# Routing the experts' tokens: every expert over all tokens, or seven sorted tiles with one expert each

## Chip, cores and metric

The kernel runs on one core of a Trainium2 chip. The metric is the device time of one execution, in microseconds, less is better. The engines are TensorE (PE), VectorE (DVE), ScalarE (ACT), GpSimd (POOL) and SyncE (SP), which only issues DMAs.

## What is computed

The input is 16 sequences ("images" below) of 512 tokens of 128 channels, all fp32. Two layers follow each other; each normalises x and adds an attention branch and a feed-forward branch to it. The part that matters here is the feed-forward branch of layer 1, a mixture of four experts of which each token uses one:

```python
def _moe(x, ln_w, ln_b, router_w, expert_wv, expert_proj):
    h = _layernorm(x, ln_w, ln_b)
    logits = h @ router_w
    expert_idx = jnp.argmax(logits, axis=-1)
    out = jnp.zeros_like(x)
    for e in range(4):                       # Dff = 512, C = 128
        gv = h @ expert_wv[e]                # 128 -> 2 x 512
        gate_raw, value = jnp.split(gv, 2, axis=-1)
        y = gate_raw * jax.nn.sigmoid(gate_raw) * value @ expert_proj[e]
        out = out + jnp.where((expert_idx == e)[..., None], y, 0.0)
    return out
```

Around it stand, per image: attention A of layer 1 (16 heads of 64, causal), a second attention B of layer 1 inside the feed-forward block (a causal convolution, 16 heads of 8 with rotary positions), whose result goes into `_moe`; and layer 2, a blockwise attention whose result reaches only the last 64 tokens in this form, and a feed-forward block with FP4-rounded operands.

## The kernel before

All weights are loaded and transposed once and stay in SBUF. Then the images pass through a software pipeline with four streams. In one iteration, image i is in `dense` (attention A and the experts), image i+1 in `ahead` (attention B, up to the routing), image i+2 in `early` (norms, convolution, queries and keys of B), and image i-1 in `behind` (layer 2). `pipeline` runs seven such iterations written out (four ahead of the loop, three behind it) and twelve as a hardware loop (`Fori`). The first and last ones lack some streams.

Each stream is cut into steps, functions with names such as `scores`, `gate`, `round_h`, and the constant list `ORDER` gives the order of all steps of an iteration. `walk` goes through that list on every engine, and each engine has its own functions for the steps in which it takes part; so the list fixes the order of the instructions on each engine, and semaphores tie the engines together. An engine does its instructions strictly in its order: a wait holds up all behind it.

An iteration in the order before: `take_over` (DVE copies the finished `xacc` of image i-1 to `xp`), `begin` (DVE copies the routing `hot` and the residual; ACT copies `h2T` to `h2Td`), then eight head pairs of attention A (`kq`, `v`, `scores`, `norm` on POOL, `z`), with attention B's `row_max` (44 units) and layer 2's attention between them. At the last pair begins the second half: `gate` and `value` 0 to 15 and `down` 0 to 3, interleaved with `ao`, with attention B's 44 `exps` and 16 `attend`, with the `early` stream and with layer 2's `round_x`, `gate1`, `up1`, `round_h` and `transpose_hq`. Gates 12 to 15 and `down` 2 and 3 stand behind the last `attend`, among `divide`, `join`, `project_y`, `ln3_*`, `down1`, `transpose3` and `route`, which end the iteration.

The experts: the activations are kept transposed, `h2Td` (128 channels x 512 tokens). Gate n = 4e + c multiplies 128 columns of expert e's weights with all 512 tokens (line 1387), value n likewise (line 1394): 32 fp32 matmuls of 512 columns an image. ACT takes the tanh (729), DVE makes (tanh + 1) x gate (980) and then x value (993), which gives `ym`. `down(e)` (1415) has 16 matmuls of 128 columns per expert, 64 an image, and `expert_acc` (1004) adds the result to `xacc` times the one-hot column `hotd[:, t, e]`. PSUM banks 0 to 2 rotate between gates and values; bank 3 holds `ao` and the downs. `route` (1128 to 1140) makes the one-hot `hot` with some ten tiny DVE operations, each linked to the one before by a semaphore wait.

Other lines of the rows: 1337 `kq`; 1359 and 1362 `scores` on PE, 718 on ACT, 1020 on DVE; 1376 `z`; 614 `norm` on POOL; 1403 `ao`; 1479/1481/760 `exps`; 1494 `attend`; 1314 any transpose of four tiles; 1599, 1604 `gate1`, `up1`; 1609 `transpose_hq`; 1616 `down1`; 1524 `route` on PE; 885 to 901 the nine operations of an FP4 rounding (`round_x`, `round_h`); 1147, 1014, 1015 `take_over` and `begin`; 543 and 549 SyncE's loads of `x`.

## Time and profile before

| | us |
|---|---|
| median of 3 runs (lowest, highest) | 3894.04 (3883.72, 3913.9) |
| the profiled execution's own time | 3885.07 |
| its span, first to last instruction | 3883.0 |
| PE busy | 3406.5 (88%) |
| DVE busy | 2506.9 (65%) |
| ACT busy | 1754.1 (45%) |
| POOL busy | 381.3 (10%) |
| mean granted clock of TensorE | 0.941 of full speed |

Busy means that an instruction of that engine was at work by the profile. PE's matmuls are pipelined and their ends modelled, so a matmul's own duration overlaps the next one's; in the chain of waits the overlap is taken out. An fp32 matmul is two instructions in the records (x2). "PEld" is the loading of the stationary operand.

### The profile page before, as it was taken

How to read it: one execution, taken by the hardware profiler on the slowest of the kernel's cores; microseconds unless marked ns; L12 is line 12 of the kernel's file. 1: busy time of each engine (PE TensorE's matmuls, PEld its weight loads, DVE VectorE, ACT ScalarE, POOL GpSimd, SP SyncE). 2: the span in 40 equal slices, each digit the busy share in tenths (PEclk: the TensorE clock that was granted, in tenths of full speed). 3: DMA queues.
4: the chain of work that ended last, by engine and by line, in shares of the span. 5: the costliest groups of instructions: out<-in, count | busy, mean ns of one | idle time of the engine just before them, and what ended most of it. 6: DMA issues, size and time to landing. Idle time of an engine off the chain costs nothing.

```text
span 3883.0 us, 62655 instructions
## 1 busy us (share of the span) xinstructions
PE 3406.5 (88%) x20319; PEld 1876.6 (48%) x20319; DVE 2506.9 (65%) x5526; ACT 1754.1 (45%) x4156; POOL 381.3 (10%) x676
## 2 busy tenths in 40 slices
PE   2689998989999898999989899898989989898864
PEld 1245455544545455454545545454555545454432
DVE  4555677657767666776766677677667767756453
ACT  0254554535454454545545454544545455454421
POOL 0000200102020010202001020200102020110201
PEclk6799999989999999999989999999999999999975
DMA  4111102020200202020020202002020200200000
GB/s 100 18 25 13 22 2 36 2 37 2 27 11 2 36 2 37 2 29 9 5 33 2 37 2 29 8 7 32 2 37 2 30 7 5 30 1 4 1 3 3
DMA packets 78817, 66.93 MB, mean 17 GB/s; under 512 B 8626, under 2 KB 75124, under 8 KB 78452
## 3 DMA queue, kind: packets, MB, share of 16 engines
q1 hardware_dynamic: 78452, 62.41, 11.2%
q8 instruction: 187, 3.06, 0.4%
q14 instruction: 178, 1.46, 0.1%
HBM read 15.47 MB, written 4.19 MB: 5 GB/s over the span
## 4 chain that ended last, share of the span: by engine, by line
PE 68%; DVE 12%; issue 8%; POOL 6%; ACT 5%; SPq 1%; DMA 1%; POOLq 0%; DVEq 0%; ACTq 0%
PE ps L1376 7%; PE ps L1394 5%; PE ps L1359 5%; PE ps L1387 5%; PE ps L1415 5%; PE ps L1494 4%; PE ps L1479 4%; PE ps L1558 3%; PE ps L1337 3%; PE ps L1580 3%; PE ps L1403 3%; DVE nma L1020 2%; PE ps L1460 2%; PE ps L1349 2%; POOL vn L614 2%
## 5 line engine op out<-in xcount | busy, mean ns | idle before, releaser
L718 ACT ACTIVATE share_a<-ps,nma 128x128 f32<-128x128 f32 (+3 forms) x1024 | 531.3, 524 | 432.3 <-DVE nma L1020 430.2
L1020 DVE TENSOR_REDUCE nma<-ps 128x2 f32<-128x256 f32 (+3 forms) x512 | 420.8, 825 | 416.0 <-PE ps L1362 408.2
L1084 DVE TENSOR_REDUCE nmx<-ps 128x1 f32<-128x384 f32 (+3 forms) x704 | 426.7, 634 | 201.9 <-PE ps L1462 198.2
L760 ACT ACTIVATE share_z<-ps 128x512 f32<-128x512 f32 (+1 forms) x704 | 367.7, 558 | 407.6 <-PE ps L1481 405.4
L614 POOL TENSOR_TENSOR vn<-va,rla 128x512 f32<-128x512 f32 x128 | 133.7, 1044 | 3060.7 <-DVE rla L976 3060.7
L1376 PE MATMUL ps<-share_a,vn 128*64 128x512 f32 (+3 forms) x2048 | 324.1, 461 | 37.1 <-POOL vn L614 35.0
L1337 PE MATMUL ps<-xnTd,wkqT 128*128 128x512 f32 x512 | 279.2, 672 | 70.1 <-issue 47.3
L729 ACT ACTIVATE share_g<-ps 128x512 f32<-128x512 f32 x256 | 153.0, 598 | 361.1 <-PE ps L1387 359.9
L1460 PE MATMUL ps<-kst,qst 96*128 96x128 bf16 (+3 forms) x1024 | 264.5, 311 | 56.1 <-DMA kst<-part 36.4
L1387 PE MATMUL ps<-h2Td,wgv 128*128 128x512 f32 x512 | 267.8, 605 | 2.8 <-ACT share_a L718 2.8
L1394 PE MATMUL ps<-h2Td,wgv 128*128 128x512 f32 x512 | 269.1, 607 | 0.0
L980 DVE SCALAR_TENSOR_TENSOR share_g<-share_g,ps 128x512 f32<-128x512 f32 x256 | 175.5, 686 | 138.5 <-ACT share_g L729 132.8
L1479 PE MATMUL ps<-qst,kst 99*128 99x512 bf16 (+3 forms) x1024 | 253.1, 303 | 12.2 <-ACT share_z L760 8.0
L1415 PE MATMUL ps<-wdn,share_a 128*128 128x128 f32 x2048 | 243.1, 277 | 21.3 <-DVE share_a L993 21.3
L1376 PEld LDWEIGHTS ps<-share_a,vn 128*64 128x64 f32 x2048 | 144.4, 143 | 234.5 <-issue 195.7
L1415 PEld LDWEIGHTS ps<-wdn,share_a 128*128 128x128 f32 x2048 | 236.6, 193 | 43.0 <-issue 33.8
L1359 PE MATMUL ps<-kq_odd 64*128 64x128 f32 (+3 forms) x1024 | 216.7, 501 | 41.6 <-ACT share_a L718 35.5
L993 DVE SCALAR_TENSOR_TENSOR share_a<-share_g,ps 128x512 f32<-128x512 f32 x256 | 175.7, 686 | 105.1 <-PE ps L1394 96.9
L1359 PE MATMUL ps<-share_g 64*128 64x128 f32 (+3 forms) x1024 | 209.7, 486 | 29.9 <-ACT share_a L718 21.3
L718 ACT ACTIVATION_READ_ACCUMULATOR share_a<-ps,nma 128x1 f32 x1024 | 202.5, 198 | 0.0
L1462 PE MATMUL ps<-up_b,ident_b 128*128 128x128 bf16 x1024 | 201.5, 225 | 0.0
L1479 PEld LDWEIGHTS ps<-qst,kst 99*128 99x128 bf16 x1024 | 99.3, 98 | 205.2 <-ACT share_z L760 98.6
(220 smaller groups left out, 5607.3 us busy)
## 6 DMA issues: line engine op xcount, KB each, us to landing
qst<-part SPq DMA_DIRECT2D x144, 128.0 KB
kst<-part SPq DMA_DIRECT2D x144, 128.0 KB
xin<-in_L_attn_x SPq DMA_DIRECT2D x16, 256.0 KB, 12.0
xk<-xn SPq DMA_DIRECT2D x16, 256.0 KB, 18.8
xres<-in_L_attn_x SPq DMA_DIRECT2D x16, 256.0 KB, 2.8
out<-xn SPq DMA_DIRECT2D x16, 256.0 KB, 11.9
wgv<-in_L_ffn_expert_wv SPq DMA_DIRECT2D x1, 2048.0 KB
qst<-share_h SPq DMA_DIRECT2D x48, 16.0 KB, 2.2
```

The source lines that it names most:

```text
L718: activation(pa[:, h % 4, OFF[t]:OFF[t] + P * (t + 1)], ps[:, b + k, 0:P * (t + 1)], ACT.Exp, bias=nma[:, h, t:t + 1], accum_out=la[:, h, ...
L760: activation(pt[:, n % 2, h % 4:h % 4 + k, 0:wd], src, ACT.Exp, scale=SCALE_B)\
L1020: v.tensor_reduce(nma[:, 2 * p:2 * p + 2, t], ps[:, b:b + 2, 0:P * (t + 1)], AX.X, ALU.max, negate=True).then_inc(amax, 1)
L1084: v.tensor_reduce(nmx[:, h:h + k, t], src, AX.X, ALU.max, negate=True).then_inc(bmax_ready, 1)
L1337: ins = mm(ps[:, b + z, :], wkqT[:, z, 2 * DA * p:2 * DA * (p + 1)], xnTd[:, :], start=True, stop=True)
L1359: mm(ps[:, b + k, 0:P * (t + 1)], kq[p % 2][rows, 0, tile(t)], kq[p % 2][rows, 1, 0:P * (t + 1)], start=True, stop=False)
L1376: ins = mm(ps[DA * k:DA * k + DA, 4, 0:P * (t + 1)], vn[:, h % 4, t, :], pa[:, h % 4, OFF[t]:OFF[t] + P * (t + 1)], start=(t == NT - 1), s ...
L1387: mm(ps[:, (2 * n) % 3, :], wgv[:, e, c * P:(c + 1) * P], h2Td[:, :], start=True, stop=True).then_inc(gate_psum, 1)
L1394: mm(ps[:, (2 * n + 1) % 3, :], wgv[:, e, DFF + c * P:DFF + (c + 1) * P], h2Td[:, :], start=True, stop=True).then_inc(value_psum, 1)
L1415: ins = mm(ps[:, 3, tile(t)], ym[:, e % 2, c, tile(t)], wdn[:, e, c, :], start=(c == 0), stop=(c == CHUNKS - 1))
L1460: mm(ps[:, b, o:o + wd], qst[0:SHIFT_ROW, h, tile(t)], kst[0:SHIFT_ROW, h, 0:wd], start=True, stop=False)
L1479: mm(ps[:, b, o:o + wd], kst[0:SHIFT_ROW + PARTS, h, tile(j)], qst[0:SHIFT_ROW + PARTS, h, j * P:T], start=True, stop=False)
```

## The change

Tokens are sorted by their expert into tiles of 128 tokens, each expert's share rounded up to whole tiles. With 512 tokens and 4 experts that is at most `SORTED` = 7 tiles, and always seven are computed. Each tile meets its own expert only, whose number is read from SBUF into a register of PE.

- `rank` (PE, end of the iteration, behind `route`): 8 small bf16 matmuls of the one-hot with a strictly triangular and an all-ones matrix give each token's rank within its expert, and each expert's total, in PSUM bank 5.
- `place` (DVE, right behind it): ten small operations, linked, give each token's row `place_i` in the sorted order and each tile's expert `expert_i`.
- `scatter` (POOL, the last step): four indirect DMAs of 128 rows of 512 bytes write the normalised activations `xh` to `h_sorted` in device memory. SyncE loads them back as `hs` (256 + 192 KB) at the start of the next iteration.
- `begin` copies `place_i` and `expert_i`; ACT's copy `h2Td` is gone.
- `sort` (behind the last `z`): 7 PE transposes of `hs`, two ACT activations with the norm's weight and bias to `hsT`, and seven `value_load`s on PE.
- Per tile j: `gate` and `value`, one matmul of 512 columns each, tokens stationary and the expert's weights moving; tanh and the two DVE operations on 128 x 512 as before; `turn`, four PE transposes and an ACT copy to `ymT`; `down`, four matmuls of 128 columns, and an ACT copy to `ysort`. Gates use banks 2 and 3, values and downs 0 and 1. Both alternate.
- `store_y` (ACT issues it) writes `ysort` to `y_sorted`; `gather` (POOL) has four indirect DMAs that fetch each token's row to `yg`; `take_over` adds `yg` to `xacc` where it copied. `acc` is gone.
- `ORDER` is new throughout. All seven tiles stand ahead of the last ten `exps`; none of the expert work is left behind `attend(3,3)`. `gate1(2)` and `up1(2)` come ahead of `exps 40`. `ln2_stats` moves behind `scores(0,3)`, `ln2_root` behind `z(0)`, `project_v` behind `scores(1,1)`; the row maxima begin behind `scores(2,0)`; the layer 2 attention is spread anew.

The diff, cut to its core:

```diff
+SORTED = NT + EXPERTS - 1
 ...
+    ("take_over",), ("begin",), ("kq", 0), ("v", 0), ("kq", 1), ("scores", 0, 0), ("v", 1), ("scores", 0, 1),
+    ("scores", 0, 2), ("scores", 0, 3), ("ln2_stats",), ("kq", 2), ("scores", 1, 0), ("scores", 1, 1),
+    ("project_v",), ("norm", 0), ("scores", 1, 2), ("z", 0), ("ln2_root",), ("v", 2), ("scores", 1, 3), ("kq",
+    3), ("ln2_apply",), ("transpose2",), ("scores", 2, 0), ("row_max", 0), ("row_max", 1), ("keys1",),
 ...
+    7), ("mix1", 1), ("z", 7), ("sort",), ("project1",), ("round_x", 0), ("load_x",), ("ln0_stats",), ("exps",
+    0), ("exps", 1), ("ln0_root",), ("ln0_apply",), ("ln1_apply",), ("ao",), ("add_ao",), ("gate", 0),
+    ("value", 0), ("gate", 1), ("exps", 2), ("exps", 3), ("value", 1), ("round_x", 1), ("turn", 0),
+    ("round_x", 2), ("round_x", 3), ("round_x", 4), ("exps", 4), ("attend", 0, 0), ("exps", 5), ("exps", 6),
+    ("down", 0), ("gate", 2), ("exps", 7), ("transpose1",), ("value", 2), ("exps", 8), ("exps", 9), ("turn",
 ...
+    26), ("round_h", 0, 0), ("round_h", 0, 1), ("round_h", 0, 2), ("round_h", 0, 3), ("attend", 2, 0),
+    ("exps", 27), ("exps", 28), ("round_h", 0, 4), ("down", 3), ("gate", 5), ("value", 5), ("exps", 29),
+    ("turn", 4), ("exps", 30), ("exps", 31), ("attend", 2, 1), ("down", 4), ("transpose_hq", 0), ("gate", 6),
+    ("gate1", 1), ("value", 6), ("turn", 5), ("up1", 1), ("round_h", 1, 0), ("exps", 32), ("down", 5),
+    ("turn", 6), ("attend", 2, 2), ("exps", 33), ("attend", 2, 3), ("round_h", 1, 1), ("down", 6),
+    ("store_y",), ("round_h", 1, 2), ("round_h", 1, 3), ("round_h", 1, 4), ("exps", 34), ("exps", 35),
+    ("transpose_hq", 1), ("exps", 36), ("exps", 37), ("gate1", 2), ("exps", 38), ("attend", 3, 0), ("exps",
+    39), ("up1", 2), ("exps", 40), ("exps", 41), ("attend", 3, 1), ("exps", 42), ("exps", 43), ("attend", 3,
+    2), ("attend", 3, 3), ("turn_x",), ("round_h", 2, 0), ("round_h", 2, 1), ("round_h", 2, 2), ("round_h", 2,
+    3), ("round_h", 2, 4), ("transpose_hq", 2), ("gather",), ("divide", 0), ("divide", 1), ("gate1", 3),
+    ("divide", 2), ("divide", 3), ("up1", 3), ("round_h", 3, 0), ("round_h", 3, 1), ("round_h", 3, 2),
+    ("round_h", 3, 3), ("join",), ("project_y",), ("round_h", 3, 4), ("transpose_hq", 3), ("ln3_stats",),
+    ("ln3_root",), ("ln3_apply",), ("down1",), ("transpose3",), ("route",), ("rank",), ("place",),
+    ("scatter",),
 ...
+                def load_sorted():
+                    sp.wait_ge(scattered, count(i, AHEAD["scattered"], 16 * NT))
+                    sp.dma_start(hs, h_sorted.rearrange("(t p) c -> p t c", p=P)).then_inc(hs_loaded, 16)
 ...
+                def scatter():
+                    pool.wait_ge(placed, count(nxt, AHEAD["placed"], 1))
+                    if type(nxt[0]) is not int or nxt[0] + nxt[1]:
+                        pool.wait_ge(scatter_turn, count(nxt, AHEAD["scatter_turn"], 0))
+                    if i is not None:
+                        pool.wait_ge(hs_loaded, count(i, DENSE["hs_loaded"], 16))
+                    nc.gpsimd.tensor_tensor(turn_s[:, :], vones[0:1, VCOLS - 1:VCOLS],
+                                            vones[0:1, VCOLS - 1:VCOLS], ALU.mult).then_inc(scatter_turn, 1)
+                    for t in range(NT):
+                        nc.gpsimd.indirect_dma_start(
+                            h_sorted, bass.IndirectOffsetOnAxis(place_i[:, t:t + 1].bitcast(U32), 0),
+                            xh[:, t, :], None).then_inc(scattered, 16)
+
+                def gather():
+                    pool.wait_ge(y_stored, count(i, DENSE["y_stored"], 16))
+                    if type(i[0]) is not int or i[0] + i[1]:
+                        pool.wait_ge(gather_turn, count(i, DENSE["gather_turn"], 0))
+                    nc.gpsimd.tensor_tensor(turn_g[:, :], vones[0:1, VCOLS - 1:VCOLS],
+                                            vones[0:1, VCOLS - 1:VCOLS], ALU.mult).then_inc(gather_turn, 1)
+                    for t in range(NT):
+                        nc.gpsimd.indirect_dma_start(
+                            yg[:, t, :], None, y_sorted,
+                            bass.IndirectOffsetOnAxis(placed_d[:, t:t + 1].bitcast(U32), 0)).then_inc(y_gathered, 16)
 ...
+                def sort():
+                    act.wait_ge(hs_psum, count(i, DENSE["hs_psum"], 1))
+                    act.wait_ge(zav_done, count(i, DENSE["zav_done"], PAIRS))
+                    activation(hsT[:, 0:T], ps[:, 0, :], ACT.Identity, bias=ln1[:, 3:4], scale=ln1[:, 2:3])\
+                       .then_inc(hsT_ready, 1)
+                    activation(hsT[:, T:SORTED * P], ps[:, 1, 0:SORTED * P - T], ACT.Identity, bias=ln1[:, 3:4],
+                               scale=ln1[:, 2:3]).then_inc(hsT_ready, 1)
+
+                def gate(j):
+                    act.wait_ge(gate_psum, count(i, DENSE["gate_psum"], j + 1))
+                    if j >= 2:
+                        act.wait_ge(moe_y, count(i, DENSE["moe_y"], j - 1))
+                    activation(sg[:, j % 2, :], ps[:, GATE_BANK[j % 2], :], ACT.Tanh, scale=0.5)\
+                       .then_inc(silu_done, 1)
+
+                def turn(j):
+                    act.wait_ge(yT_psum, count(i, DENSE["yT_psum"], j + 1))
+                    if j >= 2:
+                        act.wait_ge(down_psum, count(i, DENSE["down_psum"], j - 1))
+                    copy(ymT[:, j % 2, :, :].rearrange("p c t -> p (c t)"), ps[:, GATE_BANK[j % 2], :])\
+                       .then_inc(yT_ready, 1)
+
+                def down(j):
+                    act.wait_ge(down_psum, count(i, DENSE["down_psum"], j + 1))
+                    copy(ysort[:, j, :], ps[:, VALUE_BANK[j % 2], 0:C]).then_inc(y_ready, 1)
+
+                def store_y():
+                    act.wait_ge(y_ready, count(i, DENSE["y_ready"], SORTED))
+                    if prv is not None:
+                        act.wait_ge(y_gathered, count(prv, DENSE["y_gathered"], 16 * NT))
+                    act.dma_start(y_sorted.rearrange("(t p) c -> p t c", p=P), ysort).then_inc(y_stored, 16)
 ...
+                    v.tensor_copy(placed_d[:, :], place_i[:, :])
+                    v.tensor_copy(expert_d[:, 0:SORTED], expert_i[:, 0:SORTED])
 ...
+                def place():
+                    dve.wait_ge(rank_psum, count(nxt, AHEAD["rank_psum"], 1))
+                    if i is not None:
+                        dve.wait_ge(carried, count(i, DENSE["carried"], 1))
+                        dve.wait_ge(scattered, count(i, AHEAD["scattered"], 16 * NT))
+                    rank = ps[:, 5, 0:NT * EXPERTS].rearrange("p (t e) -> p t e", e=EXPERTS)
+                    total = ps[:, 5, NT * EXPERTS:(NT + 1) * EXPERTS]
+                    wide_lg = lg[:, :, :]
+                    begun = rb[:, :, :]
+                    link_a(v.tensor_tensor(wide_lg, total.unsqueeze(2).to_broadcast([P, EXPERTS, NT]),
+                                           sizes.rearrange("p (e n) -> p e n", e=EXPERTS), ALU.is_gt))
+                    link_a(v.tensor_tensor(begun, flat(lg).unsqueeze(1).to_broadcast([P, EXPERTS, EXPERTS * NT]),
+                                           below, ALU.mult))
+                    link_a(v.tensor_reduce(first[:, :], begun, AX.X, ALU.add))
+                    link_a(v.scalar_tensor_tensor(out=place_f[:, :, :],
+                                                  in0=first[:, :].unsqueeze(1).to_broadcast([P, NT, EXPERTS]),
+                                                  scalar=float(P), in1=rank, op0=ALU.mult, op1=ALU.add))
+                    link_a(v.tensor_tensor(place_f[:, :, :], place_f[:, :, :], hot[:, :, :], ALU.mult))
+                    link_a(v.tensor_reduce(lmax[:, :], place_f[:, :, :], AX.X, ALU.add))
+                    link_a(v.tensor_copy(place_i[:, :], lmax[:, :]), False)
+                    late = rb[:, :, :].rearrange("p a b -> p (a b)")[:, 0:SORTED * 3].rearrange(
+                        "p (n e) -> p n e", e=3)
+                    link_a(v.tensor_tensor(late, tiles.unsqueeze(2).to_broadcast([P, SORTED, 3]),
+                                           first[:, 1:EXPERTS].unsqueeze(1).to_broadcast([P, SORTED, 3]), ALU.is_ge))
+                    link_a(v.tensor_reduce(expert_f[:, 0:SORTED], late, AX.X, ALU.add))
+                    v.tensor_copy(expert_i[:, 0:SORTED], expert_f[:, 0:SORTED]).then_inc(placed, 1)
 ...
                 def take_over():
-                    dve.wait_ge(moe_acc, count(prv, DENSE["moe_acc"], EXPERTS))
+                    dve.wait_ge(ao_added, count(prv, DENSE["ao_added"], 1))
+                    dve.wait_ge(y_gathered, count(prv, DENSE["y_gathered"], 16 * NT))
                     if type(prv[0]) is not int or prv[0] + prv[1]:
                         dve.wait_ge(out_ready, count(prv, BEHIND["out_ready"], 0))
-                    link_b(v.tensor_copy(xp[:, :, :], xacc[:, :, :]))
+                    link_b(v.tensor_tensor(xp[:, :, :], xacc[:, :, :], yg[:, :, :], ALU.add))
 ...
+                expert = {}
+
+                def sort():
+                    pe.wait_ge(carried, count(i, DENSE["carried"], 1))
+                    pe.wait_ge(hs_loaded, count(i, DENSE["hs_loaded"], 16))
+                    pe.wait_ge(aexp_done, count(i, DENSE["aexp_done"], 4 * HEADS))
+                    for j in range(SORTED):
+                        ins = tr(ps[:, j // NT, tile(j % NT)], hs[:, j, :], idn)
+                    ins.then_inc(hs_psum, 1)
+                    for j in range(SORTED):
+                        expert[j] = pe.value_load(expert_d[0:1, j:j + 1], min_val=0, max_val=EXPERTS - 1)
+
+                def gate(j):
+                    if j == 1:
+                        pe.wait_ge(ao_added, count(i, DENSE["ao_added"], 1))
+                    elif j:
+                        pe.wait_ge(yT_ready, count(i, DENSE["yT_ready"], j - 1))
+                    pe.wait_ge(hsT_ready, count(i, DENSE["hsT_ready"], j // NT + 1))
+                    mm(ps[:, GATE_BANK[j % 2], :], hsT[:, tile(j)],
+                       wgv[:, bass.ds(expert[j], 1), 0:DFF].rearrange("c a f -> c (a f)"),
                        start=True, stop=True).then_inc(gate_psum, 1)
 
-                def value(n):
-                    e, c = n // CHUNKS, n % CHUNKS
-                    if n:
-                        pe.wait_ge(gate_read, count(i, DENSE["gate_read"], n))
-                    mm(ps[:, (2 * n + 1) % 3, :], wgv[:, e, DFF + c * P:DFF + (c + 1) * P], h2Td[:, :],
+                def value(j):
+                    if j < 2:
+                        pe.wait_ge(hsT_ready, count(i, DENSE["hsT_ready"], 2))
+                    else:
+                        pe.wait_ge(y_ready, count(i, DENSE["y_ready"], j - 1))
+                    mm(ps[:, VALUE_BANK[j % 2], :], hsT[:, tile(j)],
+                       wgv[:, bass.ds(expert[j], 1), DFF:2 * DFF].rearrange("c a f -> c (a f)"),
                        start=True, stop=True).then_inc(value_psum, 1)
+
+                def turn(j):
+                    pe.wait_ge(moe_y, count(i, DENSE["moe_y"], j + 1))
+                    for c in range(CHUNKS):
+                        ins = tr(ps[:, GATE_BANK[j % 2], tile(c)], ym[:, j % 2, tile(c)], idn)
+                    ins.then_inc(yT_psum, 1)
+
+                def down(j):
+                    pe.wait_ge(yT_ready, count(i, DENSE["yT_ready"], j + 1))
+                    for c in range(CHUNKS):
+                        ins = mm(ps[:, VALUE_BANK[j % 2], 0:C], ymT[:, j % 2, c, :],
+                                 wdn[:, bass.ds(expert[j], 1), c, :].rearrange("p a c -> p (a c)"),
+                                 start=(c == 0), stop=(c == CHUNKS - 1))
+                    ins.then_inc(down_psum, 1)
 ...
+                def rank():
+                    pe.wait_ge(hot_ready, count(nxt, AHEAD["hot_ready"], 1))
+                    some = lambda a, b: hot[:, a:b, :].rearrange("p t e -> p (t e)")
+                    mm(ps[:, 5, 0:NT * EXPERTS], strict_b[:, :], some(0, NT), start=True, stop=False)
+                    for t in range(1, NT):
+                        mm(ps[:, 5, t * EXPERTS:NT * EXPERTS], ones_b[:, :], some(0, NT - t), start=False,
+                           stop=(t == NT - 1))
+                    for t in range(NT):
+                        ins = mm(ps[:, 5, NT * EXPERTS:(NT + 1) * EXPERTS], ones_b[:, :], some(t, t + 1),
+                                 start=(t == 0), stop=(t == NT - 1))
+                    ins.then_inc(rank_psum, 1)
```

## Rows read from the trace of the kernel before

**Rows 1.** The page, part 2: tenths busy in 40 equal slices; PEclk the granted clock.
```profile
PE   2689998989999898999989899898989989898864
...
PEclk6799999989999999999989999999999999999975
```

**Rows 2.** SyncE's lines 543 and 549: min/median/max ns, first and last start.
```profile
L543 SPq DMA_DIRECT2D xin<-in_L_attn_x x16: 384/397/879, 42.6 to 3098.0; - x16
L543 SPq FUSED_REGOPS  x12: 51/51/58, 612.1 to 3097.8; - x12
L543 SPq MOVE xin<-in_L_attn_x x12: 35/38/38, 612.2 to 3097.9; - x12
...
DMA to landing us min/median/max: 2.7/12.0/18.0
...
L549 SPq DMA_DIRECT2D xres<-in_L_attn_x x16: 372/373/4366, 89.7 to 3329.5; - x16
```

**Rows 3.** Busy time by stretch of one iteration, and of the closing stage.
```profile
core 0: us, PE busy (x) PEld busy (x) DVE busy (x) ACT busy (x) POOL busy (x), PEclk, DMA share, GB/s
1520.34:1533.00 12.66, 9.44 (x44) 5.59 (x44) 2.60 (x14) 2.93 (x4) 0.00 (x0) 0.87 0.46 82
1533.00:1642.30 109.30, 98.76 (x585) 50.00 (x587) 73.16 (x127) 63.89 (x173) 23.82 (x42) 1.00 0.01 2
1642.30:1713.50 71.20, 70.84 (x479) 39.71 (x479) 52.42 (x118) 34.92 (x68) 0.00 (x0) 1.00 0.02 4
1713.50:1746.30 32.80, 26.37 (x165) 19.71 (x164) 26.30 (x85) 7.10 (x14) 0.00 (x0) 0.95 0.62 77
...
3733.00:3883.00 150.00, 64.65 (x146) 29.93 (x146) 50.16 (x110) 21.10 (x37) 15.48 (x34) 0.57 0.01 4
```

**Rows 4.** The chain of waits in order of time: start, us, what.
```profile
1501.08 0.86 PE ps L1387 x2
...
1520.32 9.42 issue
...
1671.67 3.57 PE ps L1415 x32
```

**Rows 5.** Timeline of PE: start, us, what, and the idle time before it.
```profile
1534.39 0.92 PE L1359 MATMUL ps<-share_g 64*128 64x384 f32 x4 [1.62 <-ACT share_a L718]
...
1662.39 0.60 PE L1314 MATMUL ps<-ident,xh 128*128 128x128 f32 x4
1662.83 1.02 PE L1394 MATMUL ps<-h2Td,wgv 128*128 128x512 f32 x2
...
1737.66 2.94 PE L1616 MATMUL ps<-wdT,share_s 128*128 128x128 f32 x24 [0.57 <-ACT share_s L822]
...
3687.78 0.76 PE L1599 MATMUL ps<-wguT,share_s 128*128 128x352 f32 x2
...
3707.84 1.92 PE L1394 MATMUL ps<-h2Td,wgv 128*128 128x512 f32 x2
...
3719.04 0.86 PE L1599 MATMUL ps<-wguT,share_s 128*128 128x352 f32 x2
```

**Rows 6.** Timeline of DVE at the restart and in the tail after it.
```profile
1529.92 0.43 DVE L1147 COPY xp<-xacc 128x512 f32<-128x512 f32 x1 [9.59 <-issue]
...
1533.07 1.02 DVE L1020 TENSOR_REDUCE nma<-ps 128x2 f32<-128x256 f32 x2
...
1732.35 0.51 DVE L885 TENSOR_REDUCE qm<-share_s 128x22 f32<-128x352 f32 x1
...
1735.96 0.53 DVE L901 TENSOR_TENSOR share_q<-share_s,qm 128x352 f32<-128x352 f32 x1
...
1744.79 0.17 DVE L1135 TENSOR_TENSOR hot<-lg,taken 128x4 f32<-128x4 f32 x1
```

**Rows 7.** Groups of instructions by line and shape: busy us, mean ns.
```profile
L993 DVE SCALAR_TENSOR_TENSOR share_a<-share_g,ps 128x512 f32<-128x512 f32 x256 | 175.7, 686 | 105.1 <-PE ps L1394 96.9 <-DVE ry L869 3.6
...
L729 ACT ACTIVATE share_g<-ps 128x512 f32<-128x512 f32 x256 | 153.0, 598 | 361.1 <-PE ps L1387 359.9
...
L1004 DVE SCALAR_TENSOR_TENSOR xacc<-ps,hotd,xacc 128x128 f32<-128x128 f32 x256 | 71.8, 345 | 1.8 <-PE ps L1415 1.8
```

257 lines of the change are left out of this document (122 added, 135 removed), and 12 rows, old and new, of the table ORDER.

## The prediction

> **What bounds the kernel now.** I read the page's slices first. TensorE (PE) is busy 8 or 9 tenths of nearly every slice at a granted clock of 0.9 [rows 1]. A loop iteration lasts 226.0 us: SyncE's line 543 runs twelve times in the loop, from 612.1 to 3097.8 us, so 2485.7 / 11 [rows 2]. One iteration, cut into stretches [rows 3]:
> - A, the restart of the loop (12.7 us) and attention A with the row maxima and layer 2 (109.3 us). PE works 9.4 and 98.8 us of it.
> - B, from the last head pair to the end of `attend(3,3)`, 71.2 us, PE busy 70.8. Nothing but less PE work shortens it.
> - C, the tail, where PE has 26.4 and DVE (VectorE) 26.3 of 32.8 us. DVE's last operation of it ends at 1744.96, 31.5 us after its start at 1713.5 [rows 6].
>
> Between a tail and the next A, DVE stands still for 9.59 us with "issue" as the cause, and the chain of waits runs through that gap with 9.42 us [rows 4, 6]. 
>
> **PE work.** The chain of waits gives times net of overlap: an fp32 matmul of 512 columns is 0.86 us (two instructions), 16 of 128 columns are 3.57 us, 0.223 each [rows 4]. Four transposes start at 1662.39 and the next work at 1662.83: 0.11 each [rows 5]. Per image the change makes
> - gate and value: 32 matmuls become 14, -18 x 0.86 = -15.5 us
> - down: 64 become 28, -36 x 0.223 = -8.0
> - transposes: 7 in `sort`, 4 in each of 7 `turn`, 35 x 0.11 = +3.9
> - `rank`: 8 small bf16 matmuls, in no row; with the transposes as the nearest, 8 x 0.11 = +0.9; ends 0 and, at 0.223, 1.8.
>
> Net -18.7 us an image. That is the ceiling, reached only where PE sets the end. The seven tiles are a constant of the code, so no data makes them fewer.
>
> **B.** PE now has 11 gates, 12 values and `down` 0 and 1 in it: 23 x 0.86 + 2 x 3.57 = 26.9 us; the other gates and downs stand in C. After, all expert work is in B: 14 x 0.86 + 28 x 0.223 + 35 x 0.11 = 22.1; `gate1(2)`, `up1(2)` (352 columns, 0.59 each by the 512's 0.86) and three transposes come forward, 1.5. B loses 3.3 us. Three costs are unknown:
> - Seven `value_load`s stand in PE's queue between `sort` and `ao`. From below: 0.035 us each, SyncE's MOVE, hidden under the transposes queued ahead, so 0. From above: 4.37 us, the longest that an instruction with an address from a register held SyncE (line 549), 30.6 in all. The nearest row is the median of such an instruction, 0.397: I take 0.4 each and no cover, +2.8 us [rows 2]. The Trainium skill (DMA: Bandwidth & Descriptors, Latency and other measured facts) gives some 600 ns as the floor of a `tensor_load`; if this is one, the estimate is 4.2 us and the sum 21 us more, which no row here shows.
> - 42 matmuls take their weights' address from a register: 51 + 38 ns of register work each [rows 2], 3.7 us on PE's sequencer. It hides behind matmuls of 0.22 to 0.86 us: 0, at most 3.7.
> - A tile becomes a chain: gate 0.86, tanh 0.60, two DVE operations of 0.69, turn 0.44, a copy of 0.60, down 0.89, a short copy: 5 us, some 6 with the handovers [rows 4, 5, 7]. Two tiles are in flight, so seven need 21 us of 70; but `down(5)`, `turn(6)`, `down(6)` stand close together. I take 2 us of stalls; 0 to 8, the upper end one more chain and a third without cover.
>
> ScalarE loses 16 tanh and the `h2Td` copy and gains 7 tanh, 2 activations, 7 copies like a tanh and 7 short ones: 10 us against 12, on an engine busy 35 of 71 us here [rows 3]: nothing. B: -3.3 + 2.8 + 2.0 = +1.5 us.
>
> **C.** DVE has few gaps here, and PE will have about 11 us of work, so DVE's list is the length. It loses four gate and four value operations (0.65 from start to start, 5.2 us), two `acc` (eight of line 1004, 2.1 with overlap), `up1(2)` (two operations of 352 columns, 1.0) and most of `round_h(2)`, nine operations, 1732.35 to 1736.40 in the fourth: 4.1 us, of which some 3.1 can run from `exps 40` on, within B. It gains the wait for `rank` (0.9) and `place`, ten small operations, each linked to the last, 0.2 us apart like those of `route` (the last takes 0.17): 2.0 [rows 6, 7]. -11.4 + 2.9 = -8.5 us. `place` stands ahead of the branch, so nothing hides it.
>
> The clock takes some back. Where PE has just waited it runs at the lower level, 1.2 GHz: after 57% of rest in the closing stage the granted clock is 0.57 (between 0.5, 1.2 GHz, and 1, 2.4 GHz), it is 0.87 at the restart, and a value matmul at the lower level takes 1.92 us, not 1.02 [rows 3, 5]. With PE at 11 of 23 us I expect that in the second half of C. On its chain are the end of `down1` (2.94 when fast), `transpose3` and `route`: +2.5 us, 0 to 7 [rows 5]. The Trainium skill (TensorE: Matmul & The Clock Gate, What's actually happening) makes this the rule, the clock is gated unless recent activity releases it, and so speaks against a change that makes PE idler; followed through all of C it gives rival 3.
>
> **A.** PE's work is as it was. DVE ran `take_over`, `begin` and the statistics ahead of the first row maximum, 1529.92 to 1533.07; now the statistics come after the first head pair, `take_over` adds two tensors (0.69 for 0.43) and `begin` has a tiny copy more: 1.5 instead of 3.15 us, -1.6. `ln2_root` moves away from where PE waited 1.62 us for ScalarE [rows 5, 6]: -0.9. Together -2.5, and from -6 to +4, since the order of the whole stretch is new.
>
> **POOL, DMA.** Four indirect DMAs in `scatter`, four in `gather`, in no row. From below 0.38 us each, from above 4.37 [rows 2]; I take 1.0, as software has to do more for them than SyncE at its 0.397. POOL needs its own restart, about DVE's 9.6 us, and `norm(0)` is wanted some 23 us after the tail: 4 + 9.6 fits. `gather` has all of C before `take_over` waits for it; loads of 256 KB land in 12 us at the median [rows 2]. Cost 0; beyond 2.3 us each, `norm(0)` is late by four times the excess. Queued behind `take_over` on DVE are `begin` and every row maximum, so a late gather would stop all of A.
>
> **Sum.** Per iteration +1.5 - 8.5 + 2.5 - 2.5 = -7.0 us. Images 0 to 14: 15 x 7.0 = 105. The last image's dense stage is bound by the layer 2 stream once the gates are gone: its four `gate1` stand at 3687.8 to 3719.0, 10.4 us apart [rows 5]; at the 7 us that DVE's six and the transposes between need, the last comes 11 earlier. Prologue, with `rank` and `place` without cover, a memset and one load: +4. 105 + 11 - 4 = 112. The profiled execution took 3885.1 us (span 3883.0), so 3773. The median of the runs shown, 3894.0, is 9 us above it; I make no correction.
>
> **Rivals.**
> 1. PE sets everything and the new order fills the holes: 16 x 18.7 = 299, 3586 us. For it: PE at 70.8 of 71.2 in B. Against: C is DVE's already, and PE rests 20 us of 226 now.
> 2. PE's sequencer: each `value_load` is a memory round trip, 2.7 us by the shortest landing [rows 2]: 18.9 in place of 2.8, an iteration 9.1 us longer than before: 3885 + 15 x 9.1 + 5 + 4 = 4030 us. It makes the kernel slower from 1.4 us a load. For it: nothing passes them in PE's queue, and `ao` stands behind them. Against: they may run beside the queued transposes.
> 3. The clock eats the gain: PE at 1.2 GHz through all of C. `down1`, `join`, `project_y`, transposes and `route`, 7 us on C's chain, double: +4.5 over the 2.5 counted, and B's tile chains stall 2 us more: -0.5 an iteration, 3870 us. It decides if the clock in C is near 0.5 throughout.
>
> **Chances and range.** Forecast, 3690 to 3840: 0.56. Between it and rival 1, and that: 0.17. Rival 3: 0.14. Rival 2: 0.13. The range, 3640 to 3890, goes halfway to rival 1 and holds rival 3. A measurement of this kernel tells about 1%. Faster by over 1% (below 3855): 0.76. Within 1%: 0.11. Slower: 0.13.
>
> **What would show it.** Right: B near 73 us, with a gap on PE behind the seven transposes; C near 25 us to DVE's last operation, DVE without gaps and PE half busy, clock under 0.95; DVE's "issue" gap near 9.6. Wrong: a PE gap over 8 us ahead of `ao`; `vn` waiting for POOL's own DMA issues; or PE idle all through B, when the tile chain and not PE is the bound.

## The result: slower by 0.9%, outside the predicted range

| | before | after |
|---|---|---|
| median of 7 runs each, us (lowest, highest) | 3905.12 (3883.72, 3913.9) | 3936.14 (3924.51, 3941.98) |
| span of the profiled execution | 3883.0 | 3928.3 |
| PE busy | 3406.5 | 3219.6 |
| DVE busy | 2506.9 | 2305.7 |
| mean granted clock | 0.941 | 0.901 |

The ratio is 1.0089 [1.0064, 1.0113]. The forecast was 3773, in a range of 3640 to 3890. The work did go: 187 us of PE and 201 us of DVE (for PE less than the ceiling of 16 x 18.7 = 299, in part since a matmul lasts longer at a lower clock, `down1` below). The time did not.

The page of the kernel after, part 2, answers to [rows 1]: more slices of 7 on PE, more 8s in the clock.

```profile
PE   2788898978889797988979788897979789797854
...
PEclk7799998989989899999989898998989899999865
```

SyncE's loads of `xin`, which answer to [rows 2]:

```profile
L589 SPq MOVE xin<-in_L_attn_x x12: 35/38/38, 635.6 to 3145.8; - x12
```

Twelve times in the loop, so an iteration is (3145.8 - 635.6) / 11 = 228.2 us; it was 226.0. I call this "the iteration" for every kernel below.

Busy time by stretch, kernel after; columns as in [rows 3]:

```profile
1539.20:1551.20 12.00, 8.74 (x36) 4.74 (x36) 1.04 (x5) 2.51 (x3) 4.10 (x5) 0.78 0.64 111
1551.20:1667.30 116.10, 103.60 (x589) 51.90 (x589) 75.43 (x140) 64.09 (x173) 24.41 (x42) 0.96 0.04 11
1667.30:1741.20 73.90, 68.88 (x491) 41.45 (x491) 48.73 (x110) 39.69 (x81) 4.25 (x6) 0.98 0.04 11
1741.20:1767.40 26.20, 15.22 (x94) 12.69 (x86) 16.87 (x69) 4.22 (x8) 0.00 (x0) 0.72 0.60 78
```

The tail (last row) shrank from 32.8 to 26.2 us, B (third row) grew from 71.2 to 73.9, and the first half (second row) from 109.3 to 116.1, with the granted clock at 0.96 instead of 1.00 in these two iterations (from z(0) to z(7), as means over the loop, 0.96 and 0.98). In the tail the granted clock is 0.72, between its two levels (0.5 and 1); it was 0.95.

The timeline of DVE, kernel after, at the end of the tail and the restart; it answers to [rows 6]:

```profile
1764.74 0.17 DVE L1225 TENSOR_TENSOR hot<-lg,taken 128x4 bf16<-128x4 f32 x1
1765.56 0.17 DVE L1242 TENSOR_TENSOR lg<-ps,tab 128x16 f32<-128x16 f32 x1 [0.65 <-PE ps L1672]
...
1767.40 0.17 DVE L1258 CAST expert_i<-expert_f 128x7 int32<-128x7 f32 x1
1777.61 0.69 DVE L1266 TENSOR_TENSOR xp<-xacc,yg 128x512 f32<-128x512 f32 x1 [10.04 <-issue]
```

The wait for `rank` is 0.65 us and `place` 2.0, as priced; the "issue" gap is 10.04 us.

The timeline of PE, kernel after: at the border from the first half to B, near the end of B, and `down1` in the tail:

```profile
1669.94 0.98 PE L1506 MATMUL ps<-ident,share_r 128*128 128x128 f32 x7
1672.66 0.43 PE L1732 MATMUL ps<-w1T,share_q 128*64 128x128 f32 x2 [1.74 <-issue]
...
1739.43 0.64 PE L1629 MATMUL ps<-share_z,vones 128*32 128x256 f32 x8 [1.18 <-issue]
1740.93 0.43 PE L1629 MATMUL ps<-share_z,vones 128*32 128x128 f32 x8 [0.86 <-ACT share_z L856]
...
1755.62 4.85 PE L1763 MATMUL ps<-wdT,share_s 128*128 128x128 f32 x24 [0.57 <-ACT share_s L920]
```

The gap of 1.74 us behind the seven transposes is where the seven `value_load`s stand. That of 1.18, with 0.86 behind it, stands between the last `attend`s, and nothing that the profile shows ends it.

The loads themselves, kernel after, line 1509 in this one iteration (min/median/max ns, first and last start):

```profile
L1509 PEldq TENSOR_LOAD <-expert_d x7: 295/297/312, 1668.1 to 1672.0; - x7
L1509 PEldq FUSED_REGOPS  x7: 146/146/157, 1668.5 to 1672.4; - x7
```

They start 3.9 / 6 = 0.65 us apart. They begin under `z(7)`, which starts at 1667.63. PE has work until 1672.66 - 1.74 = 1670.92, so 2.8 of their 7 x 0.65 = 4.5 us are covered.

### The profile page after: what moved, and what is told of

Its sections match the earlier page's. It is cut to its first block, busy times and chain, and to the rows that moved or that the text cites. A ratio compares the mean times of both kernels' runs of the same rounds, so it can differ in the third digit from the quotient of the medians.

```text
span 3928.3 us, 61348 instructions
## 1 busy us (share of the span) xinstructions
PE 3219.6 (82%) x19279; PEld 1796.0 (46%) x19279; DVE 2305.7 (59%) x5161; ACT 1779.0 (45%) x4252; POOL 525.9 (13%) x836
## 4 chain that ended last, share of the span: by engine, by line
PE 61%; DVE 14%; issue 10%; ACT 7%; POOL 6%; SPq 1%; DMA 1%; POOLq 0%; another core or an unknown queue 0%; DVEq 0%; ACTq 0%
PE ps L1495 7%; PE ps L1478 6%; PE ps L1629 4%; PE ps L1705 4%; PE ps L1614 4%; PE ps L1550 3%; DVE nma L1109 3%; PE ps L1526 3%; PE ps L1517 2%; POOL vn L662 2%; PE ps L1468 2%; PE ps L1539 2%; PE ps L1456 2%; PE ps L1763 2%; PE ps L1595 2%
## 5 line engine op out<-in xcount | busy, mean ns | idle before, releaser
L1456 PE MATMUL ps<-xnTd,wkqT 128*128 128x512 f32 x512 | 281.3, 676 | 73.9 <-issue 69.1
L662 POOL TENSOR_TENSOR vn<-va,rla 128x512 f32<-128x512 f32 x128 | 145.2, 1135 | 1175.7 <-DVE rla L1078 1175.7
L1629 PE MATMUL ps<-share_z,vones 128*32 128x512 f32 (+3 forms) x2048 | 191.7, 446 | 28.8 <-ACT share_z L856 16.2
L1616 PE MATMUL ps<-low_b,ident_b 128*128 128x128 bf16 x1024 | 195.0, 221 | 0.0
L1468 PE MATMUL ps<-wvT,xnTd 128*128 128x128 f32 x1024 | 152.2, 295 | 23.0 <-ACT share_z L793 22.5
L1705 PE MATMUL ps<-share_q,share_s 128*128 128x512 f32 x256 | 150.9, 673 | 21.8 <-ACT share_s L893 13.8
L1481 PEld LDWEIGHTS ps<-up_b,ident_b 128*128 128x128 bf16 x1024 | 58.6, 98 | 239.5 <-issue 224.6
L1456 PEld LDWEIGHTS ps<-xnTd,wkqT 128*128 128x128 f32 x512 | 97.0, 211 | 152.6 <-issue 141.9
L1468 PEld LDWEIGHTS ps<-wvT,xnTd 128*128 128x128 f32 x1024 | 136.9, 205 | 56.0 <-ACT share_z L793 33.7
## 6 DMA issues: line engine op xcount, KB each, us to landing
xk<-xn SPq DMA_DIRECT2D x16, 256.0 KB, 16.9
```

What stands on the lines that cost most here:

```text
L1456: ins = mm(ps[:, b + z, :], wkqT[:, z, 2 * DA * p:2 * DA * (p + 1)], xnTd[:, :], start=True, stop=True)
L1468: ins = mm(ps[:, 4, tile(t)], xnTd[:, tile(t)], wvT[:, 2 * DA * p:2 * DA * (p + 1)], start=True, stop=True)
L1629: ins = mm(ps[32 * k:32 * k + 32, 4, j * P:T], vones[:, c0:c0 + 32], pt[:, n % 2, k, 0:T - j * P], start=(j == 0), stop=(j == NT - 1))
L1705: mm(ps[:, 7, :], qbd[:, 2 * p:2 * p + 2, :].rearrange("c h q -> c (h q)"), k1T, start=True, stop=False)
```

## The experiments

The table sets all kernels side by side. The stretches are means over 8 to 12 loop iterations of each profile, cut at DVE's first operation of `take_over`, PE's first matmul of `z(0)` and of `z(7)`, PE's first transpose of `turn_x`, and DVE's last operation. z(7) to turn_x is the prediction's B, turn_x to DVE's end its C; the other three columns together are its A. The last column is the mean granted clock of the whole execution.

| kernel | median us | iteration | take_over to z(0) | z(0) to z(7) | z(7) to turn_x | turn_x to DVE's end | DVE's gap | clock |
|---|---|---|---|---|---|---|---|---|
| before | 3905 | 226.0 | 16.5 | 98.3 | 71.6 | 31.2 | 9.0 | 0.941 |
| after | 3936 | 228.2 | 14.4 | 105.1 | 73.8 | 25.1 | 10.6 | 0.901 |
| e1 | 3850 | 224.3 | 17.5 | 99.2 | 72.3 | 25.5 | 10.4 | 0.902 |
| e2 | 3921 | 231.3 | 15.5 | 104.7 | 71.6 | 31.2 | 9.7 | 0.936 |
| e3 | 3879 | 224.7 | 15.2 | 104.7 | 71.8 | 24.8 | 10.0 | 0.929 |
| e4 | 3854 | 223.6 | 14.3 | 105.2 | 69.2 | 25.2 | 10.6 | 0.911 |
| e5 | 3806 | 220.6 | 17.6 | 98.8 | 69.2 | 25.1 | 10.5 | 0.908 |
| e6 | 3779 | 219.1 | 17.4 | 98.4 | 69.2 | 24.9 | 10.0 | 0.930 |
| e8 | 3799 | 220.1 | 16.8 | 98.7 | 72.7 | 24.3 | 8.2 | 0.914 |
| e9 | 3859 | 223.0 | 15.7 | 104.9 | 69.0 | 24.9 | 9.7 | 0.910 |
| e10 | 3851 | 223.6 | 16.8 | 100.1 | 70.8 | 25.4 | 11.0 | 0.897 |
| e11 | 3874 | 224.7 | 14.5 | 103.7 | 70.8 | 25.7 | 10.9 | 0.908 |
| e12 | 3926 | 228.0 | 17.2 | 105.0 | 70.8 | 24.9 | 11.0 | 0.902 |
| e13 | 4024 | 235.0 | 15.3 | 105.3 | 79.5 | 25.2 | 10.5 | 0.888 |

**e1 and e2: the order of the first half.** The tail had shortened as forecast, so the loss had to come ahead of it. e1 is the changed kernel with before's list of steps up to `z(7)`; e2 is before with the changed list up to there.

```diff
 ORDER = [
-    ('take_over',), ('begin',), ('kq', 0), ('v', 0), ('kq', 1), ('scores', 0, 0), ('v', 1), ('scores', 0, 1),
-    ('scores', 0, 2), ('scores', 0, 3), ('ln2_stats',), ('kq', 2), ('scores', 1, 0), ('scores', 1, 1),
+    ('take_over',), ('begin',), ('kq', 0), ('v', 0), ('kq', 1), ('ln2_stats',), ('scores', 0, 0), ('v', 1),
+    ('scores', 0, 1), ('ln2_root',), ('project_v',), ('scores', 0, 2), ('scores', 0, 3), ('ln2_apply',),
...
```

(e1; e2 is the reverse on before.)

> The changed kernel, but with the kernel before's order of steps from take_over to the last z (gate 0 left out, sort behind z 7). The first half between the first row maximum and the last z lasts 116.1 us after the change and 109.3 before, with the same PE work. Order theory (the new order of the first half costs it): the stretch falls back to about 109.5 us and an iteration to some 221.5, the kernel to about 3928 - 15 x 6.8 = 3826 us. Clock theory (an idler tail leaves TensorE at 1.2 GHz more often, and that follows it into the first half): the order has little part, under 2 us an iteration, 3900 to 3928 us.

> The kernel before with the changed kernel's order of the first half (gate 0 just ahead of z 7, all else as before). Order theory: its first half gets about 6 us longer with the tail and the experts untouched, 3885 + 15 x 6 = 3975 us. Clock theory: the tail keeps PE busy and the clock up, so the stretch stays within 2 us of 109.3: 3885 to 3915 us.

e1: 3850.06, ratio to before 0.9865 [0.9819, 0.991]: 86 us under the changed kernel. e2: 3921.48 (3916.82 to 3961.94), ratio 1.0074 [1.0045, 1.0103], 25 us over before. Both have the order as the cause: z(0) to z(7) is 6 us shorter with the old list, 6 us longer with the new one, whichever experts the kernel has. Neither size was hit. e2's profiled execution (span 3957.0) is one of its longest, so its iteration overstates the price: 25 us of median are 1.7 an iteration.

Most of the difference stands between z(0) and z(1). Busy time of that stretch in one iteration, kernel before and then kernel after; columns as in [rows 3]:

```profile
1544.78:1566.27 21.49, 21.37 (x132) 11.56 (x132) 12.07 (x20) 11.03 (x28) 2.95 (x2) 1.00 0.00 1
```

```profile
1562.34:1587.39 25.05, 22.95 (x134) 11.95 (x134) 15.96 (x36) 11.11 (x28) 2.95 (x2) 1.00 0.00 1
```

Of the 3.6 us, 1.6 are PE work that stood ahead of z(0) in the old list (take_over to z(0) has 12.9 us of PE work before and 11.5 after, as means), and 2.0 are waits: PE idles 0.1 us there before and 2.1 after. The waits are for ScalarE's copy of z (0.7 us) and for DVE and ScalarE in layer 2's norms and attention (0.6, 0.3, 0.2 and 0.2). The granted clock is 1.00 in both. Work that only moves is gained back elsewhere; the new waits are a net loss.

**e3: matmuls that nobody reads in PE's waits.** They use PE where it rests, to keep the clock up, and change nothing else.

```diff
+                def fill(n, bank):
+                    for _ in range(n):
+                        mm(ps[:, bank, 0:P], ident_b[:, :], up_b[:, :], start=True, stop=True)
...
                 def rank():
+                    if i is not None:
+                        fill(32, 3)
                     pe.wait_ge(hot_ready, count(nxt, AHEAD["hot_ready"], 1))
```

> The changed kernel with matmuls whose results nobody reads, put ahead of PE's waits in the tail (48 of 128 bf16 columns ahead of transpose_hq 3, 32 ahead of rank, 6 ahead of join) and at the restart (24 ahead of scores 0,2); no other change. Clock theory: the granted clock of the tail rises from 0.72 to over 0.9 and of the first half from 0.96 to 1.00, down1 goes from 4.5 to 2.9 us; 4 to 7 us less an iteration, 3830 to 3870 us. Order theory: the clock in the first half rises little, and only the tail gains 1 to 2 us: 3895 to 3920 us; if the fillers only stand in the way, 3930 to 3960.

3878.84, ratio 0.9942 [0.992, 0.9963], between the two forecasts: 57 us under the changed kernel, with 110 more matmuls in each iteration (an estimated 6 us). So part of the loss may be clock. But the table shows 2.0 of its 3.5 us between z(7) and turn_x, where the 1.18 and 0.86 us waits are gone. e6 tries the fillers without those waits.

**e4: each value_load in its own gate.**

```diff
                 def sort():
...
-                    for j in range(SORTED):
-                        expert[j] = pe.value_load(expert_d[0:1, j:j + 1], min_val=0, max_val=EXPERTS - 1)
...
                 def gate(j):
+                    expert[j] = pe.value_load(expert_d[0:1, j:j + 1], min_val=0, max_val=EXPERTS - 1)
```

> The changed kernel with each value_load in its own gate step instead of seven in a row behind sort. The seven TENSOR_LOADs take 0.30 us each and PE stands 1.74 us idle behind the seven transposes. If that gap is theirs and the sequencer is ahead of PE in the second half, it goes: 1.7 us less an iteration, about 3902 us. If each load now stalls PE at its gate, nothing is won: 3920 to 3930 us.

3854.38, ratio 0.9885 [0.9844, 0.9926]: 82 us gained, far more than the 26 us of the visible gap (1.74 x 15), and far under the forecast of 3902. B falls from 73.8 to 69.2 and the waits of 1.74, 1.18 and 0.86 us are all gone. Timeline of PE, e4, the same place as 1739.43 above:

```profile
1698.51 0.91 PE L1628 MATMUL ps<-share_z,vones 128*32 128x256 f32 x16 [0.22 <-ACT share_z L856]
1700.13 0.66 PE L1433 MATMUL ps<-ident,xk 128*128 128x128 f32 x4 [0.71 <-ACT share_r L866]
```

**e5 and e6: both edits, and the fillers on top.**

```diff
 ORDER = [
-    ('take_over',), ('begin',), ('kq', 0), ('v', 0), ('kq', 1), ('scores', 0, 0), ('v', 1),
+    ('take_over',), ('begin',), ('kq', 0), ('v', 0), ('kq', 1), ('ln2_stats',), ('scores', 0, 0), ('v', 1),
...
                 def gate(j):
+                    expert[j] = pe.value_load(expert_d[0:1, j:j + 1], min_val=0, max_val=EXPERTS - 1)
```

> The changed kernel with the two edits that each gained alone: the first half up to z(7) in the order of before (alone 3850), and the value of each tile's expert loaded in that tile's own gate step instead of seven loads in a row (alone 3854). Theory 1, two separate costs in two stretches of an iteration: the gains add up, 3936 - 86 - 82 = 3768, so 3760 to 3785. Theory 2, both gains come largely through the same granted clock, which falls after one idle stretch and then falls anyway: they overlap, 3810 to 3850.

> The kernel of e5_old_half_and_loads plus the unread filler matmuls of e3_filled_tail (48 before the last transpose_hq, 32 before rank, 6 before join, 24 before scores(0,2)), which gained 57 us on the changed kernel. Theory clock: what the low clock costs is a term of its own, and a further 30 to 55 us go: 3715 to 3740 if e5 is at 3770. Theory that the fillers gained by the same holes that e5 closes: within 10 us of e5, or some 10 to 20 us above it, since the fillers take 110 x 0.06 = 6 us of PE per iteration.

e5: 3805.84, ratio 0.9775 [0.9748, 0.9803], between the two theories and 4 us from the second; e6: 3778.95, ratio 0.9707 [0.9677, 0.9737]. The gains of e1 and e4, 86 + 82, overlap by 38 us: with the other edit in place the order is worth 48 us (e4 to e5) and the loads 44 (e1 to e5). The table shows most of what they share: the hole at the end of B. z(7) to turn_x is 69.2 without loads in a row and hole, 72.3 with the loads alone (e1), 73.8 with both. Either edit removes it, 1.5 x 15 = 23 us; the other 15 are not assigned.

The loads in a row cost more than their gap, because the granted clock falls behind it. Busy time from z(7) to turn_x in two iterations of e1, with the same work:

```profile
2303.88:2376.38 72.50, 68.89 (x491) 41.30 (x492) 48.46 (x109) 40.16 (x82) 4.04 (x5) 0.98 0.04 11
2529.84:2600.72 70.88, 67.26 (x492) 39.82 (x492) 48.44 (x110) 40.15 (x82) 4.36 (x5) 1.00 0.04 12
```

Ten of e1's eleven loop iterations are like the first, with a piece at the lower clock (0.5) that begins 5.5 to 5.9 us after z(7), behind the gap; one is like the second. The kernel after has the fall in nine of eleven (B 74.0 to 74.6 us, 72.4 without it). Before, e4 and e5 never have it there, and B takes 69.2 us in every iteration of e4 and e5. So of the 3.1 us between e1 and e5, 1.65 are the gap and some 1.5 the clock.

The fillers are worth 27 us on e5 (expected 30 to 55), less than the 57 on the changed kernel, where they removed the hole too. Busy time by stretch, e5, then e6: z(0) to z(7), z(7) to turn_x, turn_x to take_over, take_over to z(0).

```profile
1520.79:1618.29 97.50, 89.44 (x542) 46.15 (x542) 65.10 (x105) 55.26 (x145) 22.77 (x41) 1.00 0.00 1
1618.29:1687.51 69.22, 67.39 (x491) 39.88 (x492) 48.41 (x109) 40.17 (x82) 4.04 (x5) 1.00 0.04 12
1687.51:1721.89 34.38, 21.39 (x111) 15.68 (x112) 17.86 (x72) 6.06 (x10) 4.11 (x5) 0.75 0.61 87
1721.89:1737.10 15.21, 10.98 (x62) 5.29 (x60) 10.99 (x38) 8.97 (x30) 1.04 (x1) 1.00 0.29 82
```

```profile
1502.73:1602.14 99.41, 92.20 (x542) 46.93 (x542) 65.13 (x104) 55.19 (x145) 22.71 (x41) 0.97 0.01 1
1602.14:1671.33 69.19, 67.36 (x492) 39.89 (x492) 48.42 (x109) 40.15 (x82) 4.04 (x5) 1.00 0.05 12
1671.33:1706.90 35.57, 19.26 (x174) 16.12 (x175) 17.87 (x71) 3.72 (x7) 4.10 (x5) 0.81 0.61 87
1706.90:1726.84 19.94, 18.62 (x108) 10.17 (x107) 11.13 (x38) 11.44 (x32) 1.04 (x1) 0.92 0.20 57
```

B is equal in both. One iteration proves little of the rest: the restart takes 15.2 us here and 19.9 there, and the fall of the clock moves from one stretch to another. The means of the table and the medians carry the verdict.

**e8: the last two tiles later.** ('gate', 6), ('value', 6), ('turn', 6), ('down', 6) and `store_y` move down the list of e5.

```diff
-    ('exps', 30), ('exps', 31), ('attend', 2, 1), ('down', 4), ('transpose_hq', 0), ('gate', 6), ('gate1', 1),
-    ('value', 6), ('turn', 5), ('up1', 1), ('round_h', 1, 0), ('exps', 32), ('down', 5), ('turn', 6),
...
+    ('up1', 1), ('round_h', 1, 0), ('gate', 6), ('exps', 32), ('down', 5), ('value', 6), ('attend', 2, 2),
...
+    ('exps', 42), ('exps', 43), ('down', 6), ('store_y',), ('attend', 3, 2), ('attend', 3, 3), ('turn_x',),
```

> The kernel of e5_old_half_and_loads with the steps of the last two expert tiles placed later, so that PE has them in the short waits between the last exps steps (in the profile of the changed kernel 0.6, 0.2, 1.2, 0.9 and 0.7 us): gate 6 before exps 32, value 6 after down 5, turn 6 after transpose_hq 1, down 6 and store_y behind exps 43. If those waits can be filled with the last tile's work, the stretch z(7) to turn_x gives back 1 to 3 us an iteration: 15 to 45 us below e5. If they are PE's waits for ScalarE that only move, or the tile's own waits for its chain take their place, it is equal to e5 within 8 us or slower.

3799.38, ratio 0.9758 [0.973, 0.9786]; 6 us under e5, within the 8 that were to count as equal. B grows by 3.5 us, and DVE's part of the tail and its gap shrink by 3.1 (0.8 and 2.3): what one stretch gives another takes. Why DVE's gap is shorter here isn't shown.

**e9: experts that don't depend on the data.**

```diff
                     for j in range(SORTED):
-                        expert[j] = pe.value_load(expert_d[0:1, j:j + 1], min_val=0, max_val=EXPERTS - 1)
+                        expert[j] = min(j // 2, EXPERTS - 1)
```

> The changed kernel with constant experts: tile j takes expert j // 2, the last one expert 3, so there are no value loads and no operand address that comes from a register. It leaves out the choice of the expert by the data. Beside it stands e4_loads_at_gates, 3854, which has seven loads, spread, and the addresses. If the spread loads and the addresses cost nothing on PE: 3845 to 3865. If each address from a register costs PE's sequencer time (7 x 6 matmuls with one): up to 59 us less, 3795. If the loads in a row cost only by what they do on the chip to the code around them, and not by their own time, it stays at 3936.

3859.34, ratio 0.9913 [0.988, 0.9946], the same as e4 within both runs' spread, and B is 69.0 against 69.2. So loads spread over the gates and 42 addresses from registers cost at most 0.2 us an iteration in B, and nothing in the median that the spread of the runs (3851 to 3871) would show.

**e10, e11 and e12: which part of the order.** All three start from e4 and change the list only. e10 has before's list up to `z(1)`, e11 the reverse, e12 has only `ln2_stats`, `ln2_root`, `project_v`, `ln2_apply` and `transpose2` back among the first scores. e12's list:

```diff
-    ('take_over',), ('begin',), ('kq', 0), ('v', 0), ('kq', 1), ('scores', 0, 0), ('v', 1), ('scores', 0, 1),
+    ('take_over',), ('begin',), ('kq', 0), ('v', 0), ('kq', 1), ('ln2_stats',), ('scores', 0, 0), ('v', 1),
+    ('scores', 0, 1), ('ln2_root',), ('project_v',), ('scores', 0, 2), ('scores', 0, 3), ('ln2_apply',),
+    ('kq', 2), ('scores', 1, 0), ('transpose2',), ('scores', 1, 1), ('norm', 0), ('scores', 1, 2), ('z', 0),
```

> The kernel of e4_loads_at_gates (new order of the first half, loads spread; 3854) with the order of before up to z(1) and the new order behind it. The whole first half in the order of before gave 3806. If the price of the new order (48 us) is that of the head pairs 0 and 1, where the mean from z(0) to z(1) is 25.1 us against 21.5 and z(1) to z(2) 16.8 against 14.8: 3806 to 3822, and the stretch z(1) to z(2) is short again too, since it inherits what is late. If it is a matter of the rest of the half (layer 2's steps between the pairs 3 to 6): 3840 to 3855.

> The mirror of e10_old_order_to_z1: the new order up to z(1), the order of before behind it. If the pairs 0 and 1 carry the price: 3840 to 3855. If the rest carries it: 3806 to 3822. If both e10 and this one lie in the middle, the price is spread over the half.

> The kernel of e4_loads_at_gates with only layer 2's chain of norms (ln2_stats, ln2_root, project_v, ln2_apply, transpose2) moved to where before has them, among scores 0 and 1; all else in the new order, kq(3) and the row_max units included. If the new order is slow because DVE has that chain behind scores 0 and 1 instead of in the waits between them (DVE is busy 7.4 us of the stretch from take_over to z(0), 10.7 before): most of the 48 us come back, 3806 to 3825. If it is where kq(3), scores(2,0) and the row_max units stand: 3845 to 3860.

3850.87, 3873.77 and 3926.07 (ratios 0.9854 [0.9825, 0.9883], 0.9928 [0.9902, 0.9953], 1.006 [1.0039, 1.0082]). None is near 3806. e10's number lies where the second theory put it, e11's in neither range, and e12 costs 72 us instead of gaining 48. The stretches say why. From take_over to z(7), e5 needs 116.4 us, e10 116.9, e11 118.2, e4 119.5, e12 122.2: the head pairs 0 and 1 do carry most of the order's price (2.6 of 3.1 us), as the first theory had it, and the norms alone, moved early, add 2.9 us to take_over to z(0) without shortening what follows. In e12 z(0) to z(1) still takes 24.9 us (e4: 25.05): the waits for the norms are gone, and others, for POOL's `vn` (1.05 us) and ScalarE's `share_a` (1.03), stand in their place. So it isn't the place of the norms alone; which of the other steps it is, no run shows. And in all three the hole at the end of B is back, 1.6 us, and takes the gain of e10 away: by medians e10 is 3.5 us under e4, while e5 is 48 under it. Timeline of PE, e10:

```profile
1700.78 0.85 PE L1628 MATMUL ps<-share_z,vones 128*32 128x384 f32 x8 [0.24 <-ACT share_z L856]
1703.61 0.64 PE L1628 MATMUL ps<-share_z,vones 128*32 128x256 f32 x8 [1.07 <-issue]
1705.11 0.43 PE L1628 MATMUL ps<-share_z,vones 128*32 128x128 f32 x8 [0.86 <-ACT share_z L856]
```

After, e10, e11, e12 and e13 have it in each of their loop iterations (PE idles 3.0 to 3.6 us of B in e10 to e12, 1.8 in e4 and e5), e1, e3, e4, e5, e6 and e9 in none, though e10 differs from e4 and e5 only in the order of steps that lie at least 70 us earlier. ScalarE is late there as well: in e10 it waits for PE 1.75 us ahead of its activation at 1702.96, in e4 0.90 at the same place. What sets it off stayed open.

**e13: fourteen loads in a row.** Each value is loaded twice.

```diff
                     for j in range(SORTED):
                         expert[j] = pe.value_load(expert_d[0:1, j:j + 1], min_val=0, max_val=EXPERTS - 1)
+                    for j in range(SORTED):
+                        twice = pe.value_load(expert_d[0:1, j:j + 1], min_val=0, max_val=EXPERTS - 1)
```

> The changed kernel (3936) with the seven loads in a row done twice, 14 in a row. A price per load (0.30 us each in the profile of the changed kernel, hidden in part by the transposes before them): the idle stretch behind them grows from 1.74 to about 3.9 us, and the time by 16 x 2.1 = 34 to, with what the clock and the queues behind it add as they did for the first seven (5.1 us an iteration for 1.74 us of idling), 80 us: 3970 to 4015. A price paid once, at the first load (waiting for the value): 3930 to 3945.

4024.23, ratio 1.0301 [1.0273, 1.033]: 88 us for seven more loads, 88 / 15 = 5.9 us an iteration, and 9 us above the range of a price per load. Timeline of PE, e13:

```profile
1698.89 0.98 PE L1506 MATMUL ps<-ident,share_r 128*128 128x128 f32 x7
1706.14 0.68 PE L1734 MATMUL ps<-w1T,share_q 128*64 128x128 f32 x2 [6.27 <-issue]
```

The gap goes from a mean of 1.79 us to 6.27: 4.48 / 7 = 0.64 us a load. The time rises by more than 16 x 4.48 = 72, so a wait here is not absorbed later. The rest fits the clock: its mean in B falls from 0.98 to 0.94.

## Why the prediction was wrong

It summed -7.0 us an iteration; measured were +2.2 (228.2 against 226.0). Nearly all of its signs of being right came: B near 73 us with a gap behind the seven transposes, C near 25 with PE 58% busy and the clock under 0.95. None of them watched the first half, where the loss is. By its own parts, from the table (their sum is +2.4, since the means leave some iterations out):

- **C, the tail: right in size, in part by luck.** -6.0 was forecast (DVE's list -8.5, clock +2.5), -6.1 came. DVE's busy time in C fell from 26.3 to 16.7 us as a mean, -9.6, but "DVE without gaps" didn't come: its idle time rose from 4.9 to 8.4 us, 5.5 of them waits for PE's transposes of `divide` (3.65) and for `route` (1.85). Those waits fill the place of the +2.5 for the clock, and the runs don't show that the clock makes them: e6's fillers raise the mean granted clock of C from 0.79 to 0.93, and C only goes from 25.1 to 24.9 us. The timeline of DVE shows `rank` at 0.65 us (priced 0.9) and `place` at 2.0 (2.0), and `down1`, 2.94 us in [rows 5], takes 4.85 after, in a tail whose granted clock is 0.72. The gap behind the list was to stay near 9.6; its mean went from 9.0 to 10.6, and single iterations have 7.5 to 10.3 before and 9.4 to 11.8 after; no run shows why. It belongs to the loop: in the iterations written out it is at most 0.2 us.
- **A: the step that failed** ("together -2.5"). -2.5 was forecast, with -6 to +4; it came to +6.3: take_over to z(0) -2.1, z(0) to z(7) +6.8, DVE's gap +1.6. I had priced what leaves the start of A, which is right (-2.1), and put what it does where it goes at nothing. The moved steps then meet the head pairs 0 to 2: z(0) to z(1) takes 25.1 us instead of 21.5 (1.6 of it moved work, 2.0 new waits of PE), z(1) to z(2) 16.9 instead of 14.8, as means. e2 shows it without any sorted tile. With the rest mended (e4 to e5) it is 3.1 us an iteration and 48 us in all. Of the other 3.2 us, 1.6 are DVE's gap. The last 1.6 stand between before and e5 as well, most of them ahead of z(0) (17.6 us for 16.5), where the mean granted clock is 0.82 in e5 and 0.92 in before; that the clock is their cause isn't shown.
- **B: +1.5 forecast, +2.2 measured, its terms off in both directions.** e9 and e4, without the loads in a row, have 69.0 and 69.2, 2.4 us less than before: PE's busy time in B falls from 71.2 to 67.4 us (-3.8, forecast -3.3), and its waits rise from 0.4 to 1.8 (+1.5, forecast 2). The loads were to cost 2.8 and cost 3.1 (e1 to e5: 72.3 to 69.2, and 44 us of median), and that this is near is luck. The 0.4 us each was too low, 0.65 is right, "no cover" was wrong, since 2.8 of 4.5 us lie under `z(7)` and the transposes, and the fall of the clock behind the gap (some 1.5 us) was no term. The Trainium skill (DMA: Bandwidth & Descriptors, Latency and other measured facts) gives about 600 ns as the floor of a `tensor_load`: 0.64 and 0.65 here agree, but an estimate by it needed the cover as well. The register addresses cost nothing measurable, as taken (e9). The rest is the hole of 1.5 us (after against e1), in no term.
- **The last image: -11 forecast, nothing came.** Its four `gate1` were to close up from 10.4 to 7 us apart once the gates are gone (that makes 3 x 3.4 = 10, not 11). Timeline of PE, kernel after, closing stage, which answers to [rows 5]:

```profile
3731.81 0.76 PE L1746 MATMUL ps<-wguT,share_s 128*128 128x352 f32 x2
...
3740.97 0.76 PE L1746 MATMUL ps<-wguT,share_s 128*128 128x352 f32 x2
...
3750.00 1.54 PE L1746 MATMUL ps<-wguT,share_s 128*128 128x352 f32 x2 [0.57 <-ACT share_s L920]
...
3760.77 1.54 PE L1746 MATMUL ps<-wguT,share_s 128*128 128x352 f32 x2 [0.57 <-ACT share_s L920]
```

  They are 9.2, 9.0 and 10.8 apart: without the gates layer 2 needs 9.0 us from one to the next where the granted clock is 0.98, and 10.8 where it is 0.50. I had counted DVE's operations and the transposes and not the handovers. From z(7) of the last image to the end it is 225.5 us, 223.4 before.
- **Rivals.** Rival 2 had the right place and the wrong path to its size: 0.65 us a load is under the 1.4 from which it was to decide. That e13, with twice the loads, comes to 4024 is no support for its 4030, which was for seven loads of 2.7 us. Rival 3 is in part true: the clock in the tail is 0.72 to 0.75, and fillers that raise the mean granted clock from 0.908 to 0.930 give 27 us (e6 against e5), some 1.7 an iteration. But by the table only 0.2 us of that lie in C; the rest is in DVE's gap (0.5) and in the first half (0.6). The Trainium skill (TensorE: Matmul & The Clock Gate, What's actually happening) says the clock follows recent activity, and the risen clock with matmuls that nobody reads agrees. Rival 1 is far off. The case that came, an order that takes back much of what the removed work gives, was not among the rivals; A's +6.3 lies beyond its upper bound of +4, the order's own 3.1 within it.

The sorted tiles by themselves do most of what was forecast, 87 us of 112: with the old order of the first half and the loads spread, e5 comes to 3806, 2.3% under before, and with the fillers e6 to 3779, 2.9% under it and 4.0% under the changed kernel (3778.95 / 3936.14, medians). Both beat both kernels.

## What to carry to other kernels

Price the order of a list as carefully as its instructions: operations taken from a waiting stretch go to another, and the sum must say what they hold up there. A change that removes work from a tuned pipeline can be undone by small new waits, here 3 us for seven loads in a row, 3 us for an order, 1.5 for a hole that nobody placed, each small beside the 18.7 us of PE work that the sum removed. Choose signs that watch every stretch that the change touches, the one priced near nothing too. Undo each part of such a change by itself before judging the whole.

## What the runs showed of the hardware

- Loading a register from SBUF on PE's queue takes 0.64 to 0.65 us from one to the next in a row; one per gate, spread, costs at most 0.2 us for all seven (B of e4 against e9).
- A gap of 1.8 us on a busy PE was followed by a piece at the lower granted clock (0.5) in ten of e1's eleven loop iterations; with the same work B took 72.5 us with it and 70.9 without.
- The "issue" gap of DVE between two iterations of the loop is 7.5 to 12.2 us in before, after, e5 and e13, and at most 0.2 between iterations written out.
- An indirect DMA of 128 rows holds POOL 0.94 to 1.03 us (eight of one iteration) and the next starts 1.3 us after it (estimated 1.0). Timeline of POOL, kernel after:

```profile
1768.46 1.03 POOL L713 DMA_INDIRECT h_sorted<-xh,place_i  x1 [0.49 <-issue]
1769.80 0.98 POOL L713 DMA_INDIRECT h_sorted<-xh,place_i  x1 [0.30 <-issue]
...
1788.92 1.04 POOL L662 TENSOR_TENSOR vn<-va,rla 128x512 f32<-128x512 f32 x1 [15.62 <-DVE rla L1078]
```

  The last line is `norm(0)`, which waits for DVE and not for POOL's own issues. POOL starts the scatter 0.4 us after the last operation of `place` starts, ahead of the loop's end; a restart of its own doesn't show.
- A hole of 1.6 us in B is there in every loop iteration of some kernels and in none of others that differ only far ahead of it. Its cause is open.
